# Turning the experts' rows in blocks on VectorE instead of on TensorE, with an exchange split between SyncE and ScalarE

## What is computed

```python
buf = jnp.zeros((E * CAP + 1, H), x.dtype).at[slot].set(x[tok])
xe = buf[:E * CAP].reshape(E, CAP, H)                 # 32 x 512 x 256
gu = jnp.einsum('ech,eoh->eco', xe, gate_up_proj)     # gate and up, 128 each
g, u = (gu[..., :I], gu[..., I:])
g = jnp.minimum(g, LIMIT)
u = jnp.clip(u, -LIMIT, LIMIT)
h = jax.nn.silu(g) * u
ye = jnp.einsum('eci,ehi->ech', h, down_proj)         # 32 x 512 x 256
...
x = x + attention(layernorm(x)) + routed(ye) + shared(layernorm(x))
```

## Time and profile before

| | |
|---|---|
| timed runs, median of 3 | 3135.45 us (3132.16 to 3135.75) |
| profiled execution, its own time | 3129.23 us |
| its span, first to last instruction | 3127.6 us |
| busy over the span | PE 3068.8 us (98%), DVE 2624.5 (84%), POOL 2102.4 (67%), ACT 1963.5 (63%) |
| mean granted TensorE clock | 0.995 of full speed |
| expert stage | 555 to 764 us after the span's start |
| attention | from 764 us on |

### The profile page before, as it was taken

The page is one execution under the profiler, slowest core; times in us unless marked ns, Lnnn a source line. Parts: engine busy times, 40 slices in busy tenths (PEclk is TensorE's granted clock), DMA queues, the critical chain, the costliest instruction groups (busy, mean ns, idle before and its releaser), DMA issues.

```text
span 3127.6 us, 54519 instructions
## 1 busy us (share of the span) xinstructions
PE 3068.8 (98%) x13443; PEld 1592.7 (51%) x13444; DVE 2624.5 (84%) x2773; ACT 1963.5 (63%) x3797; POOL 2102.4 (67%) x2156
## 2 busy tenths in 40 slices
PE   8999999999899999999999999999999999999998
PEld 3355444555455555555555555555555555555554
DVE  9622444334999999999999999999999999999995
ACT  5511420334677777777777777777777777777775
POOL 5877773011577777777777777777777777777776
PEclk9999999999999999999999999999999999999999
DMA  9821887665888888898888888988898888888887
GB/s 350 331 88 55 310 266 179 204 228 187 229 205 219 217 223 221 220 221 225 218 218 217 219 216 213 262 219 223 220 223 219 221 219 224 211 220 220 206 215 182
DMA packets 319034, 685.21 MB, mean 219 GB/s; under 512 B 120813, under 2 KB 170744, under 8 KB 318608
## 3 DMA queue, kind: packets, MB, share of 16 engines
q1 hardware_dynamic: 289808, 626.48, 76.0%
q0 software_dynamic: 29184, 58.22, 5.8%
HBM read 198.37 MB, written 159.51 MB: 114 GB/s over the span
## 4 chain that ended last, share of the span: by engine, by line
PE 69%; DMA 2%; SPq 2%; DVE 1%; issue 0%; ACT 0%; POOL 0%; DVEq 0%; ACTq 0%; POOLq 0%
PE ea_ps L1155 28%; PE ea_ps L1187 26%; PE ea_ps L1202 9%; PE ea_ps L1168 6%; DMA ea_moved<-ea_blocks 2%; SPq L976 1%; DVE ea_half_max L1282 1%; DVE ea_blocks L1299 1%; DMA out<-ahead_acc 0%; SPq L819 0%; ACT ea_scaled L1249 0%; ACT ea_prob L1237 0%; SPq L826 0%; SPq L959 0%; DVE ea_neg_max L1287 0%
## 5 line engine op out<-in xcount | busy, mean ns | idle before, releaser
L1237 ACT ACTIVATE ea_prob<-ea_ps,ea_neg_max 128x1024 f32<-128x1024 f32 x1024 | 1149.1, 1122 | 313.8 <-DVE ea_neg_max L1287 292.4
L1282 DVE TENSOR_REDUCE ea_half_max<-ea_ps 128x1 f32<-128x1024 f32 x1024 | 1201.8, 1215 | 8.5 <-PE ea_ps L1155 7.4
L1299 DVE STREAM_TRANSPOSE ea_blocks<-ea_prob 128x1792 f32<-128x1792 f32 x512 | 1043.1, 2037 | 2.9 <-DMA ea_moved<-ea_blocks 1.2
L1093 POOL COPY ea_moved<-ea_blocks 32x1792 f32<-32x1792 f32 x512 | 857.1, 1674 | 158.5 <-DVE ea_blocks L1299 49.0
L1155 PE MATMUL ea_ps<-ahead_k_hl,ahead_q_hh 128*128 128x512 f32 x2048 | 852.9, 416 | 12.7 <-ACT ea_prob L1237 12.2
L1187 PE MATMUL ea_ps<-ea_moved,ea_v 128*64 128x512 f32 x3584 | 860.0, 593 | 5.3 <-DMA ea_moved<-ea_blocks 5.2
L1155 PE MATMUL ea_ps<-ahead_k_hl,ahead_q_ll 128*128 128x512 f32 x2048 | 807.5, 394 | 0.0
L1108 POOL TENSOR_TENSOR ahead_acc<-ahead_acc,ea_scaled 128x256 f32<-128x256 f32 x512 | 375.8, 734 | 203.3 <-ACT ea_scaled L1249 67.4
L1249 ACT ACTIVATE ea_scaled<-ea_ps,ea_inv 128x256 f32<-128x256 f32 x512 | 242.2, 473 | 316.8 <-PE ea_ps L1202 312.0
L1187 PEld LDWEIGHTS ea_ps<-ea_moved,ea_v 128*64 128x64 f32 x3584 | 261.7, 137 | 351.9 <-issue 292.9
L1155 PEld LDWEIGHTS ea_ps<-ahead_k_hl,ahead_q_hh 128*128 128x128 f32 x2048 | 387.6, 189 | 85.5 <-ACT ea_prob L1237 19.5
(11 more groups left out here) (112 smaller groups left out, 2563.6 us busy)
## 6 DMA issues: line engine op xcount, KB each, us to landing
ea_moved<-ea_blocks SPq DMA_DIRECT2D x1536, 224.0 KB, 6.2
ahead_k_hl<-k_parts SPq DMA_DIRECT2D x64, 512.0 KB, 8.1
ahead_q_hh<-q_parts SPq DMA_DIRECT2D x128, 256.0 KB, 4.6
ahead_q_ll<-q_parts SPq DMA_DIRECT2D x128, 256.0 KB, 5.7
xbuf<-pr_zeros SPq DMA_DIRECT2D x32, 512.0 KB, 3.8
q_parts<-pr_part_hi SPq DMA_DIRECT2D x64, 256.0 KB, 2.4
q_parts<-pr_part_lo SPq DMA_DIRECT2D x64, 256.0 KB, 2.5
k_parts<-pr_part_hi SPq DMA_DIRECT2D x64, 256.0 KB, 2.4
```

Of the source, the lines that this page charges most:

```text
L1093: nc.gpsimd.tensor_copy(moved[r * 32:(r + 1) * 32, parity, r, :, :, :], blocks[r * 32:(r + 1) * 32, parity, r, :, :, :]).then_inc(diag_don ...
L1237: nc.scalar.activation(prob[:, i % 2, half * 1024:(half + 1) * 1024], ps[:, banks[0]:banks[1], :].rearrange("p b c -> p (b c)"), ACT.Exp, ...
L1282: nc.vector.tensor_reduce(half_max[:, i % 2, half:half + 1], ps[:, banks[0]:banks[1], :], AX.XY, ALU.max).then_inc(max_step, 1)
L1299: nc.vector.transpose(blocks[:, parity, :, j, :, :].rearrange("p c t k -> p t c k"), prob[:, (s["s"] - 1) % 2, 0:MOVED * P].rearrange("p ( ...
```

## The change

Only the rows of the first pair are still turned on TensorE. For the other fifteen pairs:

- SyncE loads the rows of both experts of a pair with one transfer of 1 MB (`load_rows`), in which each partition takes four slots that lie behind each other, so in runs of 4 KB; the results are stored in the same order. The weights have a function and semaphores of their own (`load_weights`, two transfers an expert).
- VectorE transposes the rows in 32x32 blocks, one instruction of 128x1024 an expert, into `blk` (`turn_pair`), between the two experts of the pair two before.
- Twelve transfers of 64 KB a pair carry blocks between quarters of 32 partitions from `blk` to `xeT` (`exchange`); SyncE issues six, ScalarE the other six. GpSimd copies the four quarters that stay (`diagonal`). Both tiles are there twice.
- Gate-up reads `xeT` in runs of 32 elements. The results of down lie in banks 0 and 1 for the first expert of a pair and in 2 and 3 for the second. The attention's first score, which uses banks 0 and 1, now waits for the copy of the last pair's first result.

All engines go over the pairs in the same way: two written out, a loop over the next twelve with two a turn, the last two written out.

```diff
-def load_expert(sp, io, scr, ahead, e, q):
...
+def load_rows(sp, scr, ahead, i):
+    sp.dma_start(ahead["xe"][:, :, :, :], scr["xbuf"][bass.ds(i * 2 * CAP, 2 * CAP), :]
+                 .rearrange("(q p t) d -> p q t d", p=P, q=2)).then_inc(ahead["xe_loaded"], 16)
+def load_weights(sp, io, ahead, e, q):
+    sp.dma_start(ahead["gu"][:, q, :, :].rearrange("p k o -> p (k o)"), io["gu"][bass.ds(e, 1), :, :, :]
+                 .rearrange("a p k o -> p (a k o)")).then_inc(ahead["w_loaded"][q], 16)
...
+    ways = [(a, r) for turn in range(1, QD) for a, r in zip(ACROSS, ACROSS[turn:] + ACROSS[:turn])]
...
     def sync(sp):
+        def exchange(i, b):
+            wait_apart(sp, blk_done, i, sp_waits)
+            wait_apart(sp, gu_ready, 2 * (i - 1), sp_waits)
+            for a, r in ways[:len(ways) // 2]:
+                sp.dma_start(xeT[r * 32:(r + 1) * 32, b, a, :, :, :, :],
+                             blk[a * 32:(a + 1) * 32, b, r, :, :, :, :]).then_inc(exchanged[b], 16)
+        def body(i, b):
+            if follows(i, 2):
+                wait_apart(sp, blk_done, i + 1, sp_waits)
+                load_rows(sp, scr, ahead, i + 2)
+            if follows(i, 1):
+                exchange(i + 1, 1 - b)
+                for q in range(2):
+                    wait_apart(sp, gu_ready, 2 * i + q + 1, sp_waits)
+                    wait_apart(sp, dn_kept, 2 * i + q + 1, sp_waits)
+                    load_weights(sp, io, ahead, 2 * i + 2 + q, q)
+        sp.wait_ge(turned, 2)
+        load_rows(sp, scr, ahead, 1)
...
     def gpsimd(pool):
+        def diagonal(i, b):
...
+            for r in range(QD):
+                nc.gpsimd.tensor_copy(xeT[r * 32:(r + 1) * 32, b, r, :, :, :, :],
+                                      blk[r * 32:(r + 1) * 32, b, r, :, :, :, :]).then_inc(diag_done, 1)
+        def body(i, b):
+            if follows(i, 1):
+                diagonal(i + 1, 1 - b)
+            if not isinstance(i, int) or i:
+                store(i - 1)
...
     def scalar(act):
+        def exchange(i, b):
+            act.wait_ge(blk_done, i)
+            wait_pos(act, gu_ready, 2 * (i - 1))
+            for a, r in ways[len(ways) // 2:]:
+                act.dma_start(xeT[r * 32:(r + 1) * 32, b, a, :, :, :, :],
+                              blk[a * 32:(a + 1) * 32, b, r, :, :, :, :]).then_inc(exchanged[b], 16)
+        def body(i, b):
+            if follows(i, 1):
+                exchange(i + 1, 1 - b)
+            for q in range(2):
+                if not isinstance(i, int) or i:
+                    down(i - 1, q)
+                silu(i, q)
...
     def vector(dve):
+        def turn_pair(i, b):
+            dve.wait_ge(xe_loaded, 16 * i + 16)
...
+            for q in range(2):
+                last = nc.vector.transpose(blk[:, b, :, q, :, :, :].rearrange("p r t k j -> p (t k) r j"),
+                                           xe[:, q, :, :].rearrange("p t (k r j) -> p (t k) r j", r=QD, j=32))
+            last.then_inc(blk_done, 1)
+        def body(i, b):
+            hidden(i, 0)
+            if follows(i, 2):
+                turn_pair(i + 2, b)
+            hidden(i, 1)
+        turn_pair(1, 1)
+        over_pairs(dve, body)
...
     def tensor(pe):
-        def gate_up(i, q):
+        def gate_up(i, q, b):
             n = 2 * i + q
-            pe.wait_ge(xeT_done, n + 1)
+            pe.wait_ge(w_loaded[q], 32 * i + 32)
+            if isinstance(i, int) and i == 0:
+                pe.wait_ge(xeT_done, q + 1)
+            elif q == 0:
+                pe.wait_ge(exchanged[b], SENT // 2 * (i + b))
+                pe.wait_ge(diag_done, QD * i)
...
+        def body(i, b):
+            for q in range(2):
+                if not isinstance(i, int) or i:
+                    down(i - 1, q)
+                gate_up(i, q, b)
...
@@ attention, score
+                if isinstance(tile, int) and tile == 0:
+                    pe.wait_ge(ye_done, E - 1)
```

More of the change, by code:

```diff
@@ L639, in experts_programs @@
     CT = CAP // P
-    xe, gu, dn, loaded = (ahead[name] for name in ("xe", "gu", "dn", "loaded"))
+    PAIRS = E // 2
+    SENT = QD * (QD - 1) * 16
+    xe, gu, dn, xe_loaded, w_loaded = (ahead[name] for name in ("xe", "gu", "dn", "xe_loaded", "w_loaded"))
     room = moved[:, :, :, :, :, :].rearrange("p a r j t k -> p (a r j t k)")
+    size = 2 * QD * 2 * CT * DK * 32
     def lines(n):
-        first = n * CAP
+        first = 2 * size + n * CAP
         return room[:, first:first + 2 * CAP].rearrange("p (q c) -> p q c", c=CAP)
-    xeT = room[:, 0:2 * DK * CAP].rearrange("p (q k c) -> p q k c", q=2, c=CAP)
-    gate, up, silu_g, hid = (lines(2 * DK + 2 * n) for n in range(4))
-    dn_old = lines(2 * DK + 8)[:, 0, :].rearrange("p (q d) -> p q d", d=D)
+    xeT, blk = (room[:, n * size:(n + 1) * size].rearrange("p (b a q t k j) -> p b a q t k j", b=2, a=QD, q=2, t=CT, k=DK)
+                for n in range(2))
+    gate, up, silu_g, hid = (lines(2 * n) for n in range(4))
+    dn_old = lines(8)[:, 0, :].rearrange("p (q d) -> p q d", d=D)
     ye = start["acc"][:, TILES // 2:, :].rearrange("p (q t) d -> p q t d", q=2)
@@ L662, in experts_programs, with over_pairs, follows @@
     sp_waits, pool_waits = m.sem("e_sp_waits"), m.sem("e_pool_waits")
-    def sync(sp):
[L665 to L671, removed]
+    ways = [(a, r) for turn in range(1, QD) for a, r in zip(ACROSS, ACROSS[turn:] + ACROSS[:turn])]
+    def over_pairs(eng, body):
+        for i in (0, 1):
+            body(i, i)
+        with nc.Fori(1, PAIRS // 2 - 1, engines=[eng.engine]) as j:
+            for u in range(2):
+                body(2 * j + u, u)
+        for i in (PAIRS - 2, PAIRS - 1):
+            body(i, i % 2)
+    def follows(i, n):
+        return not isinstance(i, int) or i + n < PAIRS
+    def sync(sp):
+        def exchange(i, b):
[16 more added lines that the diff above has]
+        load_rows(sp, scr, ahead, 1)
         for part in range(2):
@@ L691, in scalar, with take @@
-    def scalar(act):
-        def turn(i, q):
-            n = 2 * i + q
-            act.wait_ge(turned, n + 1)
-            nc.scalar.copy(xeT[:, q, :, :], ps[:, 0:2, :]).then_inc(xeT_done, 1)
+        def body(i, b):
[3 more added lines that the diff above has]
+                store(i - 1)
+        over_pairs(pool, body)
+        store(PAIRS - 1)
+    def scalar(act):
+        def take(q):
+            act.wait_ge(turned, q + 1)
+            for k in range(DK):
+                last = nc.scalar.copy(xeT[:, 0, :, q, :, k, :].rearrange("p a t j -> p t a j"),
+                                      ps[:, 2 * q + k, :].rearrange("p (t a j) -> p t a j", a=QD, j=32))
+            last.then_inc(xeT_done, 1)
```

114 lines of the change are left out of this document (47 added, 67 removed).

## The result

The changed kernel takes 3149.43 us (median of 20 runs, 3134.01 to 3157.16), the kernel before, timed beside it, 3132.14 us (20 runs): a ratio of 1.0051, 95% interval 1.0042 to 1.0059. It is **slower by 0.5%, 17 us**, where 16.8 us less (0.5%) was predicted, 3119 us; the time lies outside the range of 3106 to 3143. The profiled execution has a span of 3147.4 us against 3127.6.

What follows compares the result with a forecast made beforehand. TensorE bounds the expert stage before; the DMA engines were to take over. Steady pairs gain 20.4 us, the start loses 4, the end gains 0.4: 16.8 us less, 3119 us, range 3106 to 3143.

Steps and rivals of the forecast that it cites:

- The steady pair: Expert stage, two experts: 12.66 us falls to 11.2, gaining 20.4 us over 14 pairs.
- The DMA need: DMA time per expert pair: 10.6 us if longer runs pay, 11.9 if not, including 3.4 for the exchange.
- TensorE's floor: TensorE alone in the expert stage, transposes removed: 5.26 us an expert, 10.5 us a pair.
- The strided operand: Gate-up reading its moving operand in runs of 32 elements: costed at nothing.
- VectorE and GpSimd: Added work per pair: two VectorE transposes at 1.25 us each; four GpSimd copies at 0.48 to 0.55, off the path.
- The issue: Issuing transfers: SyncE 6.6 us a pair, hidden; ScalarE taken at 0.68 us each, its loop 10.5, under 11.2.
- The start: First pairs, an uncovered chain of row load, transposes and exchange: 4 us lost, between 1 and 9.
- The end: From the last experts to attention's first score: 4.7 us becomes 4.3, gaining 0.4.
- (b): DMA need of 11.9 to 12.6 us a pair: 3133 in the middle, 3138 with 12.6; chance 0.17.
- (c): ScalarE becomes the bound through slow transfer issues: with 1.2 us each, a 13.6 us pair, 3152 us; chance 0.12.
- (d): TensorE's clock falls after waits for the exchange: pair 12.95 us, 8 us lost, 3143 us; chance 0.05.
- (a): TensorE stays the bound, exchange well above 229 GB/s: pair 10.5 us, 26.6 us gained, 3109 us; chance 0.16.

Runs made afterwards that it cites:

- e4: Changed kernel with ScalarE's six exchange transfers replaced by six ScalarE copies across partition groups: 3123.0 us, 0.9971 of the kernel before.
- e3: Changed kernel loading only a quarter of each expert's weights from the third expert on, in as many issues (computes something else): 3124.7 us, ratio 0.9974 to the kernel before.
- e2: Changed kernel with SyncE's exchange issued ahead of the next rows, a second row buffer, and rows requested one pair earlier: 3138.1 us, 1.0021 of the kernel before.
- e8: Changed kernel with no exchange transfers, ScalarE copying eight blocks and GpSimd four more: 3116.0 us, 0.9944 of the kernel before.
- e10: e8 with ScalarE's eight copies spread, five before the first SiLU and three before the second: 3105.7 us, 0.9913 of the kernel before.
- e5: Changed kernel with all twelve exchange transfers issued by SyncE, none by ScalarE: 3150.5 us, 1.0063 of the kernel before.
- e12: Changed kernel with ten identity products on TensorE before its wait for the exchange: 3153.1 us, 1.0063 of the kernel before.

## Why the prediction was wrong, point by point

- **The steady pair** failed: 11.2 us were forecast, 12.84 measured, so 20.4 us of gain became 2.5 of loss. What failed is the step from need to time: "the DMA engines take over as the bound. I take 11.2 us". It allowed 0.6 us for queues that run dry, and laid no transfer on a chain. But one buffer made each load wait for the transposes of the last, and each load landed in 8.8 us beside the exchange, the stores and the weights (with half the exchange 7.3 in e4, with a quarter of the weights 6.8 in e3): landing and 4.1 to 4.7 us from load to load, in eleven of twelve steps. The start was priced with just such a chain; the steady stage was not.
- **The DMA need** lay within the 10.6 to 11.9 us of the forecast: 0.92 x 12.84 = 11.8 us in the changed kernel, 0.88 x 12.25 = 10.8 in e2. The 11.8 is at the upper end, so 0.6 of the 1.6 us missed may lie in the need; how much is not clear, as the same bytes counted 10.8 to 12.0 us from one order to another. The exchange's 3.4 us were about right: e8 without it needs 0.71 x 11.19 = 7.9, 2.9 to 3.9 less.
- The bandwidths of the earlier trace rows came from stretches with one kind of transfer each. Mixed, SyncE's and ScalarE's queues moved 26.54 + 4.92 MB in 0.717 x 160 us, 274 GB/s, where 380 to 410 for loads and 229 for the exchange were used; the stores on q0 had 12.65 MB in 0.201 x 160, 393, near the 410 used.
- **TensorE's floor** was right: 10.5 forecast, 10.32 in e10, so the transposes' removal is worth what was said once nothing else binds. To get there it took an exchange without transfers, and copies spread in ScalarE's order. The strided operand is free: 3.60 us for eight products, as contiguous before.
- **VectorE and GpSimd**: transposes 1.22 us (1.25 forecast), copies 0.61 (0.48 to 0.55). The copies are off the path; the transposes fit in VectorE's time, but their 2.4 us are a link of the rows' loop. **The issue** on ScalarE: median 0.61, longest 1.57, in the rows below (0.68 taken). Rival (c) falls: its loop is 6 x 0.61 + 6.4 = 10.1 us, and without these issues (e5) the pair was no shorter.

```profile
L763 ACTq DMA_DIRECT2D ea_moved<-ea_moved x72: 514/614/1565, 607.6 to 756.2; - x72
```
```profile
L787 DVE STREAM_TRANSPOSE ea_moved<-ahead_xe x30: 1201/1221/1246, 566.7 to 749.8; 128x1024 f32<-128x1024 f32 x30
```
```profile
L723 POOL COPY ea_moved<-ea_moved x48: 601/609/1054, 607.0 to 753.6; 32x512 f32<-32x512 f32 x48
```

- **The start**: 6.8 us lost, 4 taken, within 1 to 9. The chain was right (row load, transposes, exchange behind the next rows), and the half clock after it came as in the earlier trace rows: 0.50 from 575 to 585 us. Six issues in a row of 5.36 us in front of ScalarE's SiLU were not in it.
- **The end**: 0.4 us gained, as forecast.
- **The attention** was taken as untouched; it lost about 6 us.
- **Rivals**: nearest in mechanism was (b), a need of 11.9 to 12.6, 3133 to 3138, but a need is not what held the pair. The 17 us lost are those of (c), 3152, and the pair is near (d)'s 12.95; both are luck, as neither mechanism set the time. (a), TensorE as the bound, was reached only with no transfer of the exchange left. The last sentence of the prediction, "a row load landing so late that VectorE waits in front of its transposes", names what happened; it had no rival, no price and no chance.
- The Trainium skill, page "DMA: Bandwidth & Descriptors", section "Where 436 GB/s comes from", has SBUF to SBUF transfers bound by the fabric's 435 GB/s, by which TensorE would have stayed the bound. The changed kernel did not reach that rate either: 4.92 MB of ScalarE's transfers took 0.114 x 160 us of the 16 engines, 270 GB/s.
- The same page of the Trainium skill, section "Issuing engines are not separate DMA queues", says that issuing from several engines saves only the sequencer's time for the issue. The runs agree as far as they go: with one issuer (e5) the rows landed in 8.7 us against 8.8, and the pair was 0.4 us longer.

## What to carry to other kernels

A sum of bytes gives the least time that transfers need, not the time of a loop in which they wait for one another: write down the loop of each single buffer (landing, use, next issue) with the landing taken beside all the other traffic, and give it a rival of its own. Where a load's landing and the total traffic stand close, cutting one alone uncovers the other: two buffers alone, or less traffic alone, each gave a part. Small moves between partition groups belong on engines with idle time rather than on DMA engines that are nearly full, but in an engine's order they must stand where nobody waits behind them: the same copies, spread, were worth 10 us.

## What the runs showed that was not expected

- ScalarE copies 32x512 from one group of 32 partitions to another in 0.62 us, GpSimd in 0.61 to 0.76; twelve such copies took the place of 0.79 MB of transfers a pair.
- With the exchange on the DMA engines their share ended between 0.80 and 0.92 in every order that was tried, however the rest was arranged; the same bytes counted 10.8 us (e2) to 12.0 us (e12, 0.91 x 13.16) of DMA time a pair.
- Ten products of the identity in front of each first gate-up kept TensorE's clock at 1.00 and gained nothing: they took 2.23 us of it a pair, and the rows still took 8.3 us to land.
